# Perceiver layer on one core: the Gram tables of k and q ahead of v, and triangular systems in two stretches

## What is computed

```python
q = _silu(hs @ Wq + bq)   # (B, H=16, L=32, DK=64); k and v alike
q = q * rsqrt(sum(q * q) + 1e-6); k = k * rsqrt(sum(k * k) + 1e-6)
def step(carry, x):
    S_f = fdt * S_f; S_s = sdt * S_s
    err_f = vt - einsum('bhk,bhkv->bhv', kt, S_f)   # err_s alike with S_s
    S_f = S_f + (bt * kt) * err_f                   # S_s alike
    S_fc = _cap(S_f + rf * S_s); S_sc = _cap(S_s + rf * S_f)
    ot = fgt * einsum(qt, S_fc) + sgt * einsum(qt, S_sc)
```

## Time and profile before

| | |
|---|---|
| median of 3 runs | 1970.72 us (1969.69 to 1972.78) |
| the profiled execution: its own time | 1969.36 us |
| span of its trace | 1967.5 us |
| `project`, about | 547 to 875 us |
| one part of it (k projection to k projection) | 66.21 us |
| busy over the whole span | PE 1598.5, DVE 1177.0, ACT 706.7 us |

### The profile page before, as it was taken

How to read it: one execution, slowest core, us unless ns; L and a number is a source line. 1 busy time by engine, 2 the same in 40 slices (tenths; PEclk the granted TensorE clock), 3 DMA queues, 4 the chain that set the end, 5 groups by cost and what they waited for, 6 DMA issues and landing times. The chain is left out here.

```text
span 1967.5 us, 22035 instructions
## 1 busy us (share of the span) xinstructions
PE 1598.5 (81%) x7205; PEld 1139.8 (58%) x7205; DVE 1177.0 (60%) x2577; ACT 706.7 (36%) x1360; POOL 94.2 (5%) x262
## 2 busy tenths in 40 slices
PE   7999999999799999409600079649999999999998
PEld 3777877777677777303200056446666666666664
DVE  4355455455413777999999833335565555555555
ACT  2333333333244544300000122205555555555552
POOL 0000000000000000002111100030000000000003
PEclk9999999999899999859855569869999999999999
DMA  3211010010025135523100042045444415144104
GB/s 113 78 33 33 16 32 28 21 32 16 0 89 90 63 28 90 90 52 120 43 0 0 17 112 49 1 162 191 161 166 172 174 63 198 51 165 175 38 17 134
DMA packets 116456, 153.06 MB, mean 78 GB/s; under 512 B 47216, under 2 KB 68208, under 8 KB 116368
## 3 DMA queue, kind: packets, MB, share of 16 engines
q1 hardware_dynamic: 110640, 137.81, 23.2%
q0 software_dynamic: 2560, 8.39, 1.3%
q10 hardware_dynamic: 3168, 5.77, 0.8%
HBM read 250.32 MB, written 31.39 MB: 143 GB/s over the span
## 5 line engine op out<-in xcount | busy, mean ns | idle before, releaser
L1661 DVE TENSOR_TENSOR gl<-w_gu,gh 128x2048 fp32r<-128x2048 f32 x138 | 290.7, 2107 | 17.1 <-issue 16.9
L1596 ACT CAST gh<-w_gu 128x2048 fp32r<-128x2048 f32 x138 | 242.3, 1756 | 56.5 <-DMA w_gu<-in_up_proj 46.4
L1551 PE MATMUL bank<-w_d,hT 128*128 128x512 f32 x506 | 242.1, 597 | 8.2 <-ACT hT L1620 7.4
L1528 PE MATMUL bank<-gh,xh 128*128 128x512 f32 (+1 forms) x552 | 219.5, 398 | 11.8 <-issue 10.1
L1694 DVE TENSOR_TENSOR hid<-silu,bank 128x256 f32<-128x256 f32 x138 | 55.1, 399 | 257.6 <-ACT silu L1609 257.6
L1530 PE MATMUL bank<-gh,xl 128*128 128x512 f32 (+1 forms) x552 | 207.2, 375 | 0.0
L1529 PE MATMUL bank<-gl,xh 128*128 128x512 f32 (+1 forms) x552 | 207.2, 375 | 0.0
L1178 PE MATMUL bank<-o_v,o_outw 128*128 128x64 f32 x256 | 36.0, 310 | 179.8 <-DMA o_v<-scratch_v_rows 179.8
L1178 PEld LDWEIGHTS bank<-o_v,o_outw 128*128 128x128 f32 x256 | 36.1, 227 | 183.5 <-DMA o_v<-scratch_v_rows 180.6
L1551 PEld LDWEIGHTS bank<-w_d,hT 128*128 128x128 f32 x506 | 91.8, 189 | 81.1 <-issue 56.9
L1609 ACT ACTIVATE silu<-bank 128x256 f32<-128x256 f32 x138 | 50.5, 366 | 214.8 <-PE bank L1530 214.6
(11 more groups left out here) (288 smaller groups left out, 3073.3 us busy)
## 6 DMA issues: line engine op xcount, KB each, us to landing
w_gu<-in_gate_proj SPq DMA_DIRECT2D x46, 1024.0 KB
w_gu<-in_up_proj SPq DMA_DIRECT2D x46, 1024.0 KB
w_d<-in_down_proj SPq DMA_DIRECT2D x46, 1024.0 KB
w_gu<-in_gate_proj SPq DMA_DIRECT2D x23, 768.0 KB
w_gu<-in_up_proj SPq DMA_DIRECT2D x23, 768.0 KB
w_d<-in_down_proj SPq DMA_DIRECT2D x23, 768.0 KB
ctx_raw<-in_ctxT SPq DMA_DIRECT2D x32, 385.5 KB, 3.8
scratch_gram<-gram SPq DMA_DIRECT2D x8, 768.0 KB, 3.3
```

The source lines that it names most:

```text
L1528: pe.matmul(bank, xh[s % 2][:, k, :], hi, start=(k == 0), stop=False)
L1551: mm = pe.matmul(bank, hT[n % 2][:, c, :], w_d[:, b * (BLK // P) + c, :], start=(b == 0 and c == 0), stop=(b == NB - 1 and c == cs[-1]))
L1596: nc.scalar.copy(gh[n % RING][:, :, :, 0:bw].rearrange("p k a f -> p (k a) f"), w_gu[:, :, :, b * BLK:b * BLK + bw].rearrange("p k a f -> ...
L1661: nc.vector.tensor_tensor(gl[n % RING][:, :, :, 0:bw].rearrange("p k a f -> p (k a) f"), w_gu[:, :, :, b * BLK:b * BLK + bw].rearrange("p ...
```

## The change

PE forms the k and q products of both tiles ahead of the projection of v, and the v products behind it. `gram` loses its v table, which gets buffers, a DRAM table and a readback of its own. SP stores the gates first, reads the k and q tables back while v is projected, and the v table at the end of the part. ACT's root stands in the k projection, after the fifth activation. DVE solves rows 31 to 17 of system q-1 ahead of the k and q takes and rows 16 to 1 between these and the v takes. What needs the v table is a step of its own, `with_values`, for system q-2 behind the norms of q-1. The core of the diff:

```diff
-        gram = [sb(f"gram{s}", [P, HC, 2, 3, N]) for s in range(2)]
+        gram, gram_v = [sb(f"gram{s}", [P, HC, 2, 2, N]) for s in range(2)], [sb(f"gramv{s}", [P, HC, 2, N]) for s in range(2)]
...
-        SPLIT = 22
+        SPLIT = 16
...
+                    sp.wait_ge(pj_used, q * JOBS + 2 * HC + 1)
                     sp.wait_ge(qq_used, q + 1)
                     sp.dma_start(d["gates"][0:NG * H, cols], gates[:, :]).then_inc(gates_out, 16)
                     sp.dma_start(d["gates"][NG * H:(NG + 1) * H, cols], qq[:, :]).then_inc(gates_out, 16)
+                    for t in tiles:
+                        sp.wait_ge(pair_dve, kq_pair(t, KQ_PAIRS))
+                        sp.wait_ge(pair_act, kq_pair(t, KQ_PAIRS))
+                        sp.dma_start(d["gram_kq"][t * P:(t + 1) * P, :],
...
+                        sp.dma_start(G[rows, q, :, 0:2, :].rearrange("h i e n -> h i (e n)"),
+                                     d["gram_kq"][b * N:(b + 1) * N, :].rearrange("i (h e) -> h i e", h=H)).then_inc(loaded[q], 16)
...
+                    for i in range(BS):
+                        b = q * BS + i
+                        sp.dma_start(G[i * H:(i + 1) * H, q, :, 2, :],
+                                     d["gram_v"][b * N:(b + 1) * N, :].rearrange("i (h e) -> h i e", h=H)).then_inc(v_loaded[q], 16)
...
                     for part in (0, 1, 3, 2):
...
+                        if part == 2:
+                            pe.wait_ge(pj_used, q * JOBS + 2 * HC)
+                            kq_products(2 * q)
+                            kq_products(2 * q + 1)
...
                     pe.wait_ge(pj_used, (q + 1) * JOBS)
...
+                    v_products(2 * q)
+                    v_products(2 * q + 1)
...
                     for part in (0, 1, 3, 2):
-                        if part == 3 and q:
-                            roots(q - 1)
+                        if part == 2:
+                            for t in (2 * q, 2 * q + 1):
+                                for j in range(KQ_PAIRS):
+                                    take_kq(act, nc.scalar.copy, 1, t, j)
...
                         for c in range(HC if part < 3 else 1):
+                            if q and part == 0 and c == 5:
+                                roots(q - 1)
...
-                    tt(cf[:, :, 9], kap[:, :], diag(g, 2), ALU.mult)
...
+                def with_values(g):
+
+                    dve.wait_ge(v_loaded[g], 16 * BS)
                     dve.wait_ge(masked, 2 * W)
+                    link(tt(cf[:, :, 9], kap[:, :], diag(g, 2), ALU.mult))
...
                 for q in range(SG):
-                    if q >= 2:
-                        solve(q - 2, rest)
                     if q:
                         norms(q - 1)
+                    if q >= 2:
+                        with_values(q - 2)
                     if q:
                         prepare(q - 1)
                         solve(q - 1, first)
...
                     for t in (2 * q, 2 * q + 1):
-                        for j in range(PAIRS):
-                            take_pair(dve, nc.vector.tensor_copy, 0, t, j)
-                solve(SG - 2, rest)
+                        for j in range(KQ_PAIRS):
+                            take_kq(dve, nc.vector.tensor_copy, 0, t, j)
+                    if q:
+                        solve(q - 1, rest)
+                    for t in (2 * q, 2 * q + 1):
+                        for j in range(V_PAIRS):
+                            take_v(dve, nc.vector.tensor_copy, 0, t, j)
                 norms(SG - 1)
+                with_values(SG - 2)
                 prepare(SG - 1)
                 solve(SG - 1, range(N - 1, 0, -1))
+                with_values(SG - 1)
```

More of the change, by code:

```diff
@@ L652, in _ @@
                 for q in range(SG):
[L653 to L660, removed]
+                    tiles = (2 * q, 2 * q + 1)
                     cols = slice(q * QT, (q + 1) * QT)
-                    sp.wait_ge(pj_used, (q + 1) * JOBS)
+                    sp.wait_ge(pj_used, q * JOBS + 2 * HC + 1)
                     sp.wait_ge(qq_used, q + 1)
@@ L707, in sum_squares, with banks, kq_products, v_products @@
                               start=(c == 0), stop=(c == HC - 1)).then_inc(qq_mm, 1)
+                def banks(m):
+                    if m >= 2:
+                        pe.wait_ge(pair_dve, m - 1)
+                        pe.wait_ge(pair_act, m - 1)
+                    return [ps[2 + 2 * (m % 2)], ps[3 + 2 * (m % 2)]]
+                def kq_products(t):
+                    tc = tile_cols(t)
+                    for j in range(KQ_PAIRS):
+                        bank = banks(kq_pair(t, j))
+                        for i in range(2):
+                            for a in range(2):
+                                rows = slice(a * DK, (a + 1) * DK)
+                                mm = pe.matmul(bank[a][:, i * 2 * P:(i + 1) * 2 * P], kqT[rows, 2 * j + i, 0, tc],
+                                               kqT[rows, 2 * j + i, :, tc], start=True, stop=True)
+                        mm.then_inc(pair_done, 1)
+                def v_products(t):
+                    tc = tile_cols(t)
+                    for j in range(V_PAIRS):
+                        bank = banks(v_pair(t, j))
+                        if j < 2:
+                            for i in range(4):
+                                for a in range(2):
+                                    rows, c = slice(a * DK, (a + 1) * DK), j * 4 + i
+                                    mm = pe.matmul(bank[a][:, i * P:(i + 1) * P], vT[rows, c, tc], vT[rows, c, tc],
+                                                   start=True, stop=True)
+                        else:
+                            for c in range(HC):
+                                mm = pe.transpose(bank[c // 4][:, (c % 4) * P:(c % 4 + 1) * P], vT[:, c, tc], ident[:, :])
+                        mm.then_inc(pair_done, 1)
                 for q in range(SG):
@@ L759, in take_pair, with take_kq @@
-            def take_pair(eng, copy, a, t, j):
-                m = t * PAIRS + j
+                    v_products(2 * q)
+                    v_products(2 * q + 1)
+            def take_kq(eng, copy, a, t, j):
+                m = kq_pair(t, j)
+                eng.wait_ge(pair_done, m + 1)
+                if j == 0 and t >= 2:
+                    eng.wait_ge(gram_out[t % 2], 16 * (t // 2))
+                bank = ps[2 + 2 * (m % 2) + a].rearrange("p (i e b n) -> p i e b n", i=2, e=2, b=BT)
+                for b in range(BT):
+                    rows = slice(b * N, (b + 1) * N)
+                    ins = copy(gram[t % 2][rows, 2 * j:2 * j + 2, a, :, :], bank[rows, :, :, b, :])
+                ins.then_inc(pair_dve if a == 0 else pair_act, 1)
@@ L761, in take_pair, with take_v @@
+            def take_v(eng, copy, a, t, j):
+                m = v_pair(t, j)
                 eng.wait_ge(pair_done, m + 1)
@@ L772, in take_pair @@
                     rows = slice(b * N, (b + 1) * N)
[L773 to L779, removed]
+                    ins = copy(gram_v[t % 2][rows, j * 4:(j + 1) * 4, a, :], bank.rearrange("p (i b n) -> p i b n", i=4, b=BT)[rows, :, b, :])
                 ins.then_inc(used, 1)
@@ L813, in _ @@
                     for t in (2 * q, 2 * q + 1):
-                        for j in range(PAIRS):
-                            take_pair(act, nc.scalar.copy, 1, t, j)
+                        for j in range(V_PAIRS):
+                            take_v(act, nc.scalar.copy, 1, t, j)
                 roots(SG - 1)
```

59 lines of the change are left out of this document (27 added, 32 removed).

## The result

| | median us | lowest to highest | runs | ratio to before, 95% |
|---|---|---|---|---|
| before | 1971.01 | 1969.69 to 1972.78 | 4 | |
| after | 1956.68 | 1955.29 to 1957.31 | 4 | 0.9925 [0.9913, 0.9937] |

The change takes 14.3 us off. The profiled execution of after took 1957.31 us; its span is 1955.5 us, 12.0 less than before. In b_norest and b20 they are those of the kernel before.

What follows compares the result with a forecast made beforehand. TensorE was taken to pace the later parts of `project` and VectorE the tail behind them. Tail -21.9, parts +4.4 and clock +2.5 sum to -15.0 us, forecast 1955.7 us, range 1951 to 1962.

Steps and rivals of the forecast that it cites:

- tail: VectorE's work alone behind the last part of `project`: from 61.5 us to 39.6 us, giving back 21.9 us.
- part 0: First part of `project`, nothing else on VectorE: 65.97 us, 0.24 us less than now.
- lateness, parts 1 to 3: Rows 16 to 1 on VectorE end 1.8 us after the v products could be taken: each part 1.55 us longer.
- clock: TensorE idle 2.1 us in parts 1 to 3: up to 1.7 us a dip, one and a half dips taken, 2.5 us.
- E: Moment the takes of a part end; forecast at A+21.2 in part 0 and A+23.0 in parts 1 to 3.
- A: Moment the eight pairs of k and q takes of a part end; forecast at K+45.74.
- K: Start of a part of `project`'s loop, from which times within the part are counted.
- The covers: Slack in a part: 5.7 us less 0.4 before the k and q takes; 1.2 us for TensorE behind the root.
- The readback: Reading k and q tables back takes the old 16.4 us (bounds 10.9 and 16.4), ending at A+19.7; pieces count, not bytes.
- The rival in which the v tables end the tail: Last values step waits for 128 B pieces; slower than before from E+55, 1985 us at four times the row; chance 0.04.
- further stall in the parts: Rival: root, late readback or slower products stall each of three parts, 3 to 9 us in all, 1959 to 1965; chance 0.18.
- No lateness: Rival: rows 16 to 1 fit under the v projection, so 4.4 and 2.5 us go: -22.8, 1948 us; chance 0.06.

Runs made afterwards that it cites:

- b_norest: The kernel before with the second stretch of system 2 (rows 22 to 1) left out of the tail; 1969.22 us, ratio 0.999.
- b20: The kernel before with SPLIT = 20 instead of 22, rows 22 and 21 moved into the first stretch; 1969.29 us, ratio 0.9993.
- fill: The changed kernel with four unread products of 256 columns put into TensorE's gap in each of parts 1 to 3; 1950.21 us, ratio 0.9896.
- s14: The changed kernel with SPLIT = 14 instead of 16, rows 16 and 15 moved into the first stretch; 1950.23 us, ratio 0.9891.
- root_late: The changed kernel with ScalarE's root put back ahead of the gates, as in the kernel before; 2011.79 us in one run.
- s15: The changed kernel with SPLIT = 15 instead of 16, one row more in the first stretch; 1948.92 us, ratio 0.9889.
- s22: The changed kernel with the old split, SPLIT = 22 instead of 16; 1982.48 us, ratio 1.0049.

## Why the prediction held, step by step

The time on record was 1955.7 us, the measured median is 1956.68. By terms, in this execution:

| term | predicted | measured |
|---|---|---|
| tail | -21.9 | -21.91 |
| part 0 | -0.24 | -0.14 |
| lateness, parts 1 to 3 | +3 x 1.55 | +3 x 1.5 (fill) |
| clock | +1.5 dips x 1.7 = 2.5 | +3.5, 3 dips together |
| sum | -15.0 | -14.0 by these terms, -13.9 in `project` |

- **The tail.** Right in its size and in its parts: norms at once, values, a preparation of 4.9 us, the solve, values. The recurrence starts at 861.34 and not near 858, because the last take comes at E = 821.16: the tail starts later, it is not longer. The 858 was a slip of mine beside that: it is 875.35 - 17.5, without the clock's 2.5 us, and my sum gives 860.4. The break-even of the v tables, E+55, leaves the clock out in the same way; by the sum it is E+52.6, and four times the row would have given about 1987 us. Neither enters the forecast.
- **DVE late at the v takes.** Right. A was set at K+45.74 and is K+45.7 (659.11); the second stretch ends at K+61.9 as worked out; PE's gap was to be 2.1 us and is 2.08, 2.09 and 2.08. Only the other end was 0.2 us off: the first v take could start at A+14.6 (s14) and not A+14.4, which makes DVE 1.6 us late and not 1.8, and leaves the part's length as it was forecast, since DVE sets it. That the takes of before and the solve's rows keep their times in the new order was the assumption under this, and it held.
- **The clock: the mis-sized term.** I had three dips in seven gaps of 1.64 us and took one and a half of three. All three came. The loss was set at 1.7 us a dip, as of dense matmuls; it is 1.2 (3.5 / 3). PE's products take 1.6 us longer at each place, but in fill PE waits 0.40 us for DVE ahead of the second turned copy, and in parts 1 and 2 of after that wait is gone: the longer products lie under DVE's takes by so much. In the attention stage, where PE never waits behind the gap, a dip costs its full 1.6 us (in before, the gaps follow each other by 60.24 us with a dip and by 58.66 without). Two errors of opposite sign, 1.0 us net: that the sum came so near is in part luck. The Trainium skill ("TensorE: Matmul & The Clock Gate", HAM oscillation) tells of a wait in every step that costs the clock in every step. Its kernel waits about 3 to 5 us each time, so it was no rule for a gap of 2.1 us, and I should not have taken one from it: the three dips of three in after look like it, the two of three in root_late and the one in three of the attention stage (below) do not. The sum that I gave for three dips was 2.5 us worse than mine, and it came 1.0 worse, for the price just given.
- **The covers.** The root ends at K+10.88 (624.31), as set; ACT is at the sixth activation at K+12.19; the k projection takes 13.98 us with no wait for ACT, so the cover of 1.2 us was enough. Ahead of the takes I had 5.7 less 0.4 us of cover; idle before `qq` and before the first take are 4.67 + 0.61 = 5.28.
- **The readback: wrong, without effect on the time.** I kept the old 16.4 us for the k and q tables and gave the v tables as much, at 4.0 ns a piece. In part 0 the k and q readback moved data from 596.7 to 606.6 us, 9.9 us, against 13.9 in before. My 16.4 ran from the first issue (now 595.76) until DVE went on, 1.6 us behind the last data in before; on that measure it is about 12.5 us now, an estimate, between my bounds of 10.9 and 16.4. The v tables moved from 616.3 to 621.2, about 5 us, and the last data came 7 us behind that part's E (614.39), not 20. The step that failed is that time goes by pieces; it goes by bytes (below). The rival in which the v tables end the tail had its chance from that step, and was further off than I had it.
- **The rivals.** No further stall in the parts: DVE waits for no table, and PE for no activation in the k projection. No lateness was the other one; it is what s14 then made true, by other means, and the forecast for it (-22.8 us) is what s14 gives in the trace: 305.6 against 327.96 is -22.3.

What stays open: why one gap of about 2 us costs the clock and another does not (below), and what makes the stretch behind `project` up to 4.8 us longer in one execution than in another, which is more than any single term of the parts.

## What to carry to other kernels

When work is moved from a tail under a loop, set the split by the cover on both sides of it: here 5.3 us of idle time stood ahead of the k and q takes while DVE was 1.6 us late behind them, and two rows (out of 31) moved across were worth another 6.5 us by the medians, 8.4 in the traces. Before moving the work that ends a tail, look at what lands just ahead of its end: taking 23.6 us out of it gave 1.3 us until the readback was made earlier as well. And a wait of 2 us on TensorE can cost more than itself, here 1.2 us of clock on top of 1.6 us of lateness: fill it or shrink it.

## What the runs showed of the hardware

**Gaps and the granted clock.** Gaps of 2.08 and 2.09 us ahead of L758 were followed by a stretch at 1.2 GHz in three of three cases in after, and in two of three in root_late; in the third (695.94) the granted clock stayed at 1.00. PE in root_late, part 1 and a window of it, then part 2:

```profile
695.94 1.09 PE L758 MATMUL bank<-ident,vT 128*128 128x128 f32 x8 [2.09 <-DVE gramv L817]
697.16 2.06 PE L754 MATMUL bank<-vT 64*128 64x128 f32 x32
...
783.02 1.85 PE L758 MATMUL bank<-ident,vT 128*128 128x128 f32 x8 [2.08 <-DVE gramv L817]
784.80 2.90 PE L754 MATMUL bank<-vT 64*128 64x128 f32 x32
```

```profile
695.00:701.00 6.00, 4.53 (x51) 4.05 (x52) 5.18 (x17) 3.04 (x11) 0.00 (x0) 1.00 0.35 134
```

Gaps of 0.45 and 0.78 us (s14, s15) left the clock at 1.00 in every part, and those of 9.5 us (s22) cost it in all three.

The seven gaps of 1.64 us of the attention stage stand in all ten traces, with the same work around them. Behind 23 of the 70 the clock falls, and always behind every third: the first, fourth and seventh in three traces (before one of them), the second and fifth in six (after one of them), the third and sixth in one. So the same gap at the same place costs the clock in one execution and not in another. PE of after, 6 us behind the first gap, which dips in the earlier trace rows, and 6 us behind the second:

```profile
136.00:142.00 6.00, 6.00 (x33) 1.00 0.01 4
194.30:200.30 6.00, 6.00 (x25) 0.72 0.07 23
```

More of the longer gaps cost the clock, but their length alone does not decide: when the gap comes matters as well, and what sets that no run here shows.

**Readbacks of small pieces go by bytes.** Three readbacks of 4096 pieces each, with the gates' 96 KB beside the first two: 384 B in before, 256 B in after (k and q), 128 B in after (v). The DMA view of before over 619.14 to 635.50, then of after over 594 to 612 and 615 to 640, each number the GB/s of a fortieth of the window:

```profile
GB/s 0 0 52 224 208 105 148 150 135 95 110 137 116 120 101 129 115 135 99 115 139 137 100 107 141 137 106 109 138 131 113 106 136 109 73 52 0 0 0 0
```

```profile
GB/s 391 428 237 0 0 0 174 145 109 195 78 159 95 140 95 121 112 91 125 108 93 124 108 90 130 106 92 61 0 0 0 0 0 0 0 0 0 191 373 410
...
GB/s 387 413 166 123 130 130 131 106 120 97 0 0 0 0 0 0 0 0 0 0 0 13 0 0 0 26 0 0 0 0 0 0 0 0 0 0 0 0 0 0
```

In before 34 slices of 0.41 us, 13.9 us; in after 22 of 0.45 us, 9.9 us, and, behind the last store, about 8 of 0.625 us, 5 us: 3.4, 2.4 and 1.2 ns a piece, at much the same rate, 105 to 120 GB/s (bytes over that time). The eight issues of the last one took 4.09 us on SP's queue, so that one may be paced by them and not by its bytes; in either case 128 B pieces cost no more than 1.3 ns each. The Trainium skill ("DMA: Bandwidth & Descriptors", Specifications) says that transfers under 512 B cost a read-modify-write. I had read from it that the pieces count whatever they hold; these rows, all under 512 B, do not show that: between 384 and 128 B the time falls with the bytes.
